# Spreading the fields of a compressed interaction network over partitions: DMA from a DRAM scratch in place of selection matmuls, with 17 split tiles in place of 23

## The reference

```python
for idx, (W, b) in enumerate(params):
    z = jnp.einsum('bhd,bkd,hks->bsd', x0, xk, W) + b[None, :, None]
    z = jax.nn.relu(z)
    if idx != n_layers - 1:
        half = z.shape[1] // 2
        xk = z[:, :half, :]
        direct.append(z[:, half:, :])
    else:
        direct.append(z)
logit = jnp.sum(jnp.concatenate(direct, axis=1), axis=-1)
```

## Time and profile before

| what | us |
|---|---|
| median of 3 runs | 2996.9 (2995.06 to 2997.92) |
| span of the profiled execution | 2989.2 |
| PE busy | 2879.6 (96%) |
| DVE busy | 2752.8 (92%) |
| ACT busy | 1724.0 (58%) |
| POOL busy | 1628.9 (54%) |
| bytes moved | 16.17 MB, 5 GB/s over the span |

### The profile page before, as it was taken

The page is one execution under the profiler, slowest core; times in us unless marked ns, Lnnn a source line. Parts: engine busy times, 40 slices in busy tenths (PEclk is TensorE's granted clock), DMA queues, the critical chain, the costliest instruction groups (busy, mean ns, idle before and its releaser), DMA issues.

```text
span 2989.2 us, 32998 instructions
## 1 busy us (share of the span) xinstructions
PE 2879.6 (96%) x9666; PEld 1773.7 (59%) x9666; DVE 2752.8 (92%) x2461; ACT 1724.0 (58%) x1733; POOL 1628.9 (54%) x644
## 2 busy tenths in 40 slices
PE   1999999999999999999999999999999999999988
PEld 0566665666666666666566666666666666666646
DVE  3599999999999999999999999999999999999983
ACT  0466655566655556665556666555666555566634
POOL 7448194783819566381965639396572948700000
PEclk9899999999999999999999999999999999999999
DMA  2000000000000000000000000000000000000000
GB/s 63 4 3 3 3 3 5 2 5 2 2 3 2 5 3 4 1 3 3 2 5 3 4 1 2 4 2 5 3 4 1 2 5 2 5 0 0 2 19 29
DMA packets 35184, 16.17 MB, mean 5 GB/s; under 512 B 17023, under 2 KB 33520, under 8 KB 35008
## 3 DMA queue, kind: packets, MB, share of 16 engines
q0 software_dynamic: 19968, 5.15, 2.0%
q1 hardware_dynamic: 11752, 7.61, 1.0%
q10 hardware_dynamic: 3367, 2.48, 0.3%
HBM read 13.09 MB, written 2.11 MB: 5 GB/s over the span
## 4 chain that ended last, share of the span: by engine, by line
PE 82%; ACT 6%; issue 5%; DVE 4%; ACTq 0%; POOL 0%; DMA 0%; SPq 0%; DVEq 0%
PE zacc_a L781 31%; PE zacc_b L781 26%; PE side_a L827 6%; PE side_b L827 6%; PE zacc_a L814 6%; PE zacc_b L814 5%; DVE prod L681 3%; ACT spread L508 2%; ACT high L527 1%; ACT direct L491 1%; ACT maps L490 1%; ACT maps L489 1%; DVE low L654 1%; DVE sums L690 1%; PE side_a L836 0%
## 5 line engine op out<-in xcount | busy, mean ns | idle before, releaser
L429 POOL DMA_INDIRECT landed<-in_tbl,rows_id x624 | 1527.4, 2448 | 203.8 <-issue 199.7
L681 DVE TENSOR_TENSOR prod<-spread,maps 128x1024 f32<-128x1024 f32 (+1 forms) x1280 | 1506.2, 1212 | 29.1 <-PE zacc_b L814 16.3
L527 ACT ACTIVATE high<-prod 128x1024 fp32r<-128x1024 f32 (+2 forms) x736 | 776.7, 1055 | 752.1 <-DVE prod L681 504.9
L654 DVE TENSOR_TENSOR low<-prod,high 128x1024 fp32r<-128x1024 f32 (+1 forms) x672 | 814.6, 1212 | 22.8 <-ACT high L527 22.7
L781 PE MATMUL zacc_a<-prod,w_plain 128*128 128x512 f32 (+2 forms) x1536 | 720.6, 594 | 0.0
L781 PE MATMUL zacc_b<-prod,w_plain 128*128 128x512 f32 (+2 forms) x1536 | 718.2, 593 | 0.0
L450 POOL TENSOR_TENSOR mark<-mark 128x1 f32<-128x1 f32 x15 | 101.1, 6743 | 770.7 <-DVE rows_split L608 697.0
L781 PEld LDWEIGHTS zacc_a<-prod,w_plain 128*128 128x128 f32 (+2 forms) x1536 | 289.7, 189 | 231.1 <-issue 201.2
L781 PEld LDWEIGHTS zacc_b<-prod,w_plain 128*128 128x128 f32 (+2 forms) x1536 | 289.1, 189 | 230.5 <-issue 197.0
L508 ACT ACTIVATE spread<-side_a 128x1024 f32<-128x1024 f32 x320 | 326.8, 1021 | 101.2 <-PE side_a L827 100.4
L508 ACT ACTIVATE spread<-side_b 128x1024 f32<-128x1024 f32 x320 | 327.0, 1022 | 89.3 <-PE side_b L827 78.1
(11 more groups left out here) (110 smaller groups left out, 1811.8 us busy)
## 6 DMA issues: line engine op xcount, KB each, us to landing
landed<-in_tbl,rows_id POOLq DMA_INDIRECT x624
features<-feat ACTq DMA_DIRECT2D x16, 128.0 KB, 1.7
spread<-features SPq DMA_DIRECT2D x4, 512.0 KB, 5.3
spread<-in_pick SPq DMA_DIRECT2D x1, 856.8 KB
spread<-in_W_top SPq DMA_DIRECT2D x1, 512.0 KB, 4.1
rows_id<-in_ids SPq DMA_DIRECT2D x16, 19.5 KB, 1.7
spread<-in_W_top SPq DMA_DIRECT2D x2, 128.0 KB, 2.8
spread<-in_W_top SPq DMA_DIRECT2D x1, 256.0 KB, 2.9
```

The source lines that it names most:

```text
L429: nc.gpsimd.indirect_dma_start(out=landed[:, f, :], out_offset=None, in_=tables[f], in_offset=bass.IndirectOffsetOnAxis(ap=rows_id[:, f:f ...
L527: nc.scalar.activation(high[0:rows, h, :], prod[0:rows, p, :], ACT.Copy).then_inc(s_round, 1)
L654: nc.vector.tensor_tensor(to, whole, top, ALU.subtract).then_inc(s_lowv, 1)
L681: nc.vector.tensor_tensor(to, spread[0:rows, t, :], maps[0:rows, :], ALU.mult).then_inc(s_prod, 1)
```

## The change

The selection matmuls, `pick`, the split of the rows and the ACT copies of spread tiles are gone. PE now turns the gathered rows in plain float32 (`turn_x`), both chunks of a group together at position 13 of an even turn, and ACT copies each to `x` (`copy_x`, position 15). SP then writes x to two scratch tensors in DRAM (`write_x`, position 16 of the even turn, for the two chunks that come two and three turns later): `x_copies`, 8 copies of even and odd fields, and `x_periods`, 4 copies of x in a row. From there SP loads what the products need: `load_first` (x_thrice in three DMAs, and the shifted x of u = 0 to 3) after the last product of layer 0, one `load_shifted` for each of u = 4 to 6, when a buffer of the ring of four is free, and ten `load_spread` of two tiles (1 MB) each, whose source repeats each row for 8 partitions. DVE multiplies the shifted x from SBUF. `PLAN` has 17 V tiles (7, 3 and 7 in the three parts) and 30 F tiles. GpSimd gathers all of a group from position 16 of an even turn on.

```diff
-PLAN = "FVFVFVFFVFVFFVFVFVFVFVFFFVFVFVFVFVVFVFVVFVFVFVV"
+PLAN = "FVFFVFFVFFVFFVFFFVFV" "FVFVFVF" "FVFFVFFVFFVFFVFFFVFV"
-LAG = 2
-AHEAD = 4
-LOW_ROWS_AT, COPY_ROWS_AT = 42, 40
-TURN_AT, THRICE_AT = 3, 9
+TURN_AT, COPY_AT, WRITE_AT, GATHER_AT = 13, 15, 16, 16
...
+    x_copies = nc.dram_tensor("x_copies", (GROUPS, 2, 2, COPIES, N1, COLS), f32, kind="Internal").ap()
+    x_periods = nc.dram_tensor("x_periods", (GROUPS, 2, PERIODS, FIELDS, COLS), f32, kind="Internal").ap()
...
-        pick = sb("pick", [SPLIT, PICK_W], f32r)
-        ident_r = sb("ident_r", [128, 128], f32r)
+        ident = sb("ident", [128, 128])
...
-            with sp.Fori(1, GROUPS) as g:
-                sp.wait_ge(s_gather, g * (16 * FIELDS))
-                sp.dma_start(rows_id[:, :], ids[bass.ds(g * ROWS, ROWS), :]).then_inc(s_ids, 16)
...
+            def write_x(n):
+
+                odd = n.odd
+                sp.wait_ge(s_x, n.count(1, 1))
+                for h in range(2):
+                    to = x_copies[bass.ds(group_of(n), 1), odd, h, :, :, :].rearrange("g i t c -> (g t) i c")
+                    sp.dma_start(to, x[h:EVEN:2, odd:odd + 1, :].to_broadcast([N1, COPIES, COLS])
+                                 ).then_inc(s_written[odd], 16)
+                to = x_periods[bass.ds(group_of(n), 1), odd, :, :, :].rearrange("g k f c -> (g f) k c")
+                sp.dma_start(to, x[0:FIELDS, odd:odd + 1, :].to_broadcast([FIELDS, PERIODS, COLS])
+                             ).then_inc(s_written[odd], 16)
+
+            def period(n, first, rows):
+                flat = x_periods[bass.ds(group_of(n), 1), n.odd, :, :, :].rearrange("g k f c -> (g k f) c")
+                return flat[first:first + rows, :]
+
+            def load_shifted(n, u):
+                rows = rows_of(N1 + u)
+                sp.dma_start(shifted[0:rows, u % RING0, :], period(n, PER0 * u, rows)).then_inc(s_shifted[u], 16)
+
+            def load_first(n):
+
+                sp.wait_ge(s_written[n.odd], n.group(48, 48))
+                for s in range(PER0):
+                    sp.dma_start(x_thrice[s * FIELDS:(s + 1) * FIELDS, :], period(n, FIELDS - s, FIELDS)
+                                 ).then_inc(s_thrice, 16)
+                for u in range(RING0):
+                    load_shifted(n, u)
+
+            def load_spread(n, q):
+                src = x_copies[bass.ds(group_of(n), 1), n.odd, :, :, PIECE * q:PIECE * (q + 1), :]
+                src = src.rearrange("g h i t c -> (g h i) (t c)")
+                to = spread[:, PIECE * q:PIECE * (q + 1), :].rearrange("p t c -> p (t c)")
+                sp.dma_start(to, src.unsqueeze(1).to_broadcast([2 * COPIES, COPIES, PIECE * COLS])
+                             ).then_inc(s_spread[q], 16)
+
+            def emit(turn, j):
+                nxt, after = turn.shift(1), turn.shift(2)
+                if turn.fixed and turn.number() == -1 and j == 0:
+                    write_x(nxt)
+                    write_x(after)
+                    sp.wait_ge(s_gather, 16 * FIELDS)
+                    sp.dma_start(rows_id[:, :], ids[ROWS:2 * ROWS, :]).then_inc(s_ids, 16)
+                    load_first(nxt)
+                if j == WRITE_AT and not turn.odd and after.real():
+                    write_x(after)
+                    write_x(turn.shift(3))
+                    if turn.shift(4).real():
+                        sp.wait_ge(s_gather, after.group(16 * FIELDS, 16 * FIELDS))
+                        sp.dma_start(rows_id[:, :], ids[bass.ds(after.group(ROWS, ROWS), ROWS), :]).then_inc(s_ids, 16)
+                u = j - N1 - 1 + RING0
+                if RING0 <= u < N0 and nxt.real():
+                    sp.wait_ge(s_square, nxt.count(N0, u - RING0 + 1))
+                    load_shifted(nxt, u)
+                if j == SQUARED[-1] and after.real():
+                    sp.wait_ge(s_square, nxt.count(N0, N0))
+                    load_first(after)
+                q = (j - LAST[0]) // PIECE
+                if j in LAST and (j - LAST[0]) % PIECE == PIECE - 1 and nxt.real():
+                    if turn.real():
+                        sp.wait_ge(s_prod, n_prod(turn, j) + 1)
+                    elif q == 0:
+                        sp.wait_ge(s_prep, 1)
+                    load_spread(nxt, q)
+
+            turns(sp, emit, GROUPS - 2)
...
+                fetched = turn.shift(4)
+                if j == GATHER_AT and not turn.odd and fetched.real():
+                    pool.wait_ge(s_ids, fetched.group(16, 16))
+                    pool.wait_ge(s_turned, fetched.count(1, 0))
+                    pool.wait_ge(s_mark, fetched.group(1, -1))
+                    nc.gpsimd.tensor_tensor(mark[:, 0:1], mark[:, 0:1], mark[:, 1:2], ALU.add).then_inc(s_mark, 1)
+                    gather()
...
-            def high_rows():
-
-                nc.scalar.activation(rows_split[:, :, 0:FIELDS].rearrange("p d f -> p f d"), landed[:, :, :], ACT.Copy
-                                     ).then_inc(s_rowh, 1)
-
-            def spread_tile(turn, t):
-
-                nxt = turn.shift(1)
-                rows = rows_of(t)
-                if turn.fixed and turn.number() == -1 and t == 0:
-                    act.wait_ge(s_prep, 1)
-                act.wait_ge(s_side, n_side(nxt, SPREAD_X + t) + 1)
-                if turn.real():
-                    act.wait_ge(s_prod, n_prod(turn, N1 + N0 + t) + 1)
-                nc.scalar.activation(spread[0:rows, t, :], side(nxt, SPREAD_X + t)[0:rows, :], ACT.Copy
-                                     ).then_inc(s_spread, 1)
+            def copy_x(n):
+
+                act.wait_ge(s_turned, n.count(1, 1))
+                if not n.fixed or n.number() > 1:
+                    act.wait_ge(s_written[n.odd], n.group(48, 0))
+                nc.scalar.activation(x[0:FIELDS, n.odd, :], sides[n.odd][0:FIELDS, :], ACT.Copy).then_inc(s_x, 1)
...
+                if j == COPY_AT and not turn.odd and turn.shift(2).real():
+                    copy_x(turn.shift(2))
+                    copy_x(turn.shift(3))
+                if nxt.real() and j == N1 + N0 - 1 + LZ:
+                    take(turn, 0)
...
-                        dve.wait_ge(s_thrice, nxt.count(1, 1))
-                    dve.wait_ge(s_side, n_side(nxt, SQUARE_X + u) + 1)
-                    nc.vector.tensor_tensor(to, side(nxt, SQUARE_X + u)[0:rows, :], x_thrice[0:rows, :],
+                        dve.wait_ge(s_thrice, nxt.count(16 * PER0, 16 * PER0))
+                    dve.wait_ge(s_shifted[u], nxt.count(16, 16))
+                    nc.vector.tensor_tensor(to, shifted[0:rows, u % RING0, :], x_thrice[0:rows, :],
                                             ALU.mult).then_inc(s_square, 1)
...
-                    dve.wait_ge(s_spread, turn.count(N1, t + 1))
+                    if t % PIECE == 0:
+                        dve.wait_ge(s_spread[t // PIECE], turn.count(16, 16))
...
-                def pick_fields(use, first, n):
-
-                    for hf in range(2):
-                        cols = slice(hf * BANK, (hf + 1) * BANK)
-                        done = nc.tensor.matmul(side(nxt, use)[0:n, cols], pick[:, first:first + n],
-                                                x_split[:, cols], start=True, stop=True)
-                    done.then_inc(s_side, 1)
...
+            def turn_x(n):
+
+                if not n.odd:
+                    pe.wait_ge(s_gather, n.group(16 * FIELDS, 16 * FIELDS))
+                if not n.fixed or n.number() > 1:
+                    pe.wait_ge(s_x, n.count(1, -1))
+                nc.tensor.matmul(sides[n.odd][:, 0:2], ident[:, :], ident[:, 0:2], start=True, stop=True)
+                for d in range(CHAN):
+                    done = nc.tensor.transpose(sides[n.odd][0:FIELDS, d * ROWS:(d + 1) * ROWS],
+                                               landed[:, :, n.odd * CHAN + d], ident[:, :])
+                done.then_inc(s_turned, 1)
...
+                if j == TURN_AT and not turn.odd and turn.shift(2).real():
+                    turn_x(turn.shift(2))
+                    turn_x(turn.shift(3))
```

More of the change, by code:

```diff
@@ L211, in build @@
         s_zero = sem("s_zero")
-        s_pick = sem("s_pick")
         s_prep = sem("s_prep")
@@ L708, in emit @@
                     low_part(then, i)
-                if j == LOW_ROWS_AT and not turn.odd and turn.shift(2).real():
-                    low_rows(turn.group(1, 2))
                 if turn.real() and j == N1 + LZ + 2:
```

168 lines of the change are left out of this document (44 added, 124 removed).

## The result

The changed kernel takes **3188.28 us** (median of 4 runs, 3169.29 to 3219.68) against 2997.41 for the kernel before on the same chip: **1.059 times, 95% interval 1.051 to 1.067, slower**. The prediction said 2870 us, 4% faster, with 2710 to 3090 as its range; the time lies outside. One of the four runs, 3219.68 us, was a slow one and is not in the ratio; the median of the other three is 3170.5.

The account below looks back on a forecast made before the run. PE and DVE, both nearly full, were taken as the bound, with a DMA wait of 4.5 us a chunk added. 196 + 31 x 83.5 + 79.8 + 7.7 = 2872, about 2870 us, 4% faster; range 2710 to 3090.

Parts of the forecast that it names:

- PE 77.5: PE's time per chunk, from 87.3 us, with selections and old turn off, six F tiles and new turn on.
- DVE 76.7: DVE's time per chunk, against 84.1 us before: 47 products, 17 low parts in place of 23, two reduces.
- 79 without a DMA wait: Chunk time in us with both engines within 1 us of each other, feeding each other through 8 buffers; floor 77.5.
- PE's turn: PE turning the gathered rows in plain float32: 2.0 us a chunk taken, against 0.55 for the old turn.
- The slack of 9.3 us: Even turns: time from the writes' issue until DVE needs the shifted x of u = 4, 15.9 less 6.6 us.
- The time of the writes: Even turns: 3.9 MB in 10.1 to 19.3 us plus 4.1 for the load; DVE waits 4.9 to 14.1, 9 taken.
- The third rival: The DMA is the bound (chance 0.17), by low rate or too few engines; with ten on x_copies writes, 3100 us.
- The start: Time to layer 2's first relu: from 202.9 to about 196 us, first product at 77 to 87, layer 1 about 104.
- The second rival, the lock-out: DVE's two-input SBUF operations lock GpSimd out, so gathers come late: 89.1 us a chunk, 3046 in all; chance 0.19.
- signs for the end of a lock-out: On GpSimd's gathers: two of 20.64 and 34.94 us ended at a DVE product out of PSUM and at a DVE gap.
- The spread loads: Loads of 1.05 MB taking 2.7 to 5.2 us, due about 30 us after issue, so hidden unless the queue runs full.
- the end: Time after layer 2's last relu, taken to keep its 79.8 us.

Follow-up runs that it names:

- after_one_copy: The changed kernel, but x_copies holds one copy of each row in place of eight and a spread load is two DMAs; 2852.47 us, ratio 0.956.
- more20: The changed kernel with ids loaded ahead of the six writes and 2.62 MB more written from 20 rows in every even turn; 3428.23 us, ratio 1.146.
- one_copy: The changed kernel with ids ahead, one chunk's writes at position 24 of every turn, load_first behind spread loads, x_copies of one copy; 2743.38 us, ratio 0.912.
- let_in: The kernel of one_copy with a short DVE reduce behind the products at positions 6, 13, 33 and 40 of every chunk; 2821.6 us, ratio 0.943.
- let_in_memset: The kernel of one_copy with a one-column DVE memset behind the products at the same four positions as let_in; 2737.52 us, ratio 0.914.

## Why the prediction was wrong, by its steps

- **PE 77.5, DVE 76.7, 79 without a DMA wait: nearly right.** Without the wait the chunk took 77.1. PE's turn was two pieces of 1.1 us for the group, from 1655.14 to the next matmul at 1657.10, 2.0 for two chunks and so 1.0 a chunk, not 2.0. That PE's and DVE's rings hide each other's waits was priced too high by 2 us.
- **The slack of 9.3 us: right.** The first write was issued at 1657.53, and DVE was through with the product before at 1667.5: 10.0 us.
- **The time of the writes: the step that failed.** The sum took 10.1 to 19.3 us from 386 and 202 GB/s, both reached by loads, and chose a wait of 9 by the middle. Writes and load took 36.7 us. By the rates of after_one_copy and more20, 12 GB/s an engine, the 2.6 MB from 20 rows need 22 us on ten engines and the 1.3 MB from 39 rows 8 us on thirteen: 30, and a load of 4 behind them make 34 of the 36.7. The third rival gave this case: writes of 29 us, a wait of 24, a chunk of 91, 3100 us. Measured were 26.7 and 91.5; that the chunk agrees so well is in part luck, since 79 was 2 too high and the late gathers, which that rival did not have, put 2.5 on. The Trainium skill's rule (DMA: Bandwidth & Descriptors, how many engines a DMA uses) is what the rival rested on, and the traces agree with it, as above. It should have had the sum and not a part of 0.17: nothing in the trace of before spoke against ten engines, and the case for the middle was the width of its own bounds.
- **The start: wrong by 59 us.** Predicted 196, measured 255.3. Layer 0's first product came at 101.0 us and not at 77 to 87, and layer 1's matmuls at 136.8 and not at 104: the chain there runs over the same writes and ten loads of 1 MB at 221 GB/s (from 116 to 162 us, the engines busy throughout), where 386 had been taken as possible. That is 33 of the 59. Another 22.6 is the wait at 209.56, which the prediction left out of the start though by its own mechanism it stands there too. With one copy it is 207.5, and with the ids ahead as well 199.9.
- **The second rival, the lock-out: its mechanism is there, its size was not.** 30 gathers over 20 us (996 us together) stand against 22 (654 us) in the kernel before, which hid them all. The late gathers cost 77 us, 2.5 a chunk, not 5.6, and went when the ids moved ahead of the writes, so that half of the gathers fell into DVE's waits. Its signs for the end of a lock-out, a gap of DVE or a product out of PSUM, are borne out by the traces; that a reduce between two-input operations lets GpSimd in is not, for the long ones.
- **The spread loads: right in the changed kernel, and near the edge.** The changed kernel's waits for them are 30 us in 7 places. They were priced by size; reading 16 rows eight times each costs a quarter of the queue's time against 128 rows, which shows once the 26.8 us are gone.

From the sum: 59 for the start, 31 x (91.5 - 83.5) = 248, less 2 for the end and 12 more between the median and this span than the 7.7 taken, make the 317 us from 2872 to 3188. The 12 are scatter: the profiled execution's own time is 1.8 us above its span, and the median of the four runs 17.8 above that time.

## What to carry to other kernels

- Before a transfer is priced by a rate, see from what shape that rate came: writes from 20 rows ran at 120 GB/s on ten engines and from 32 rows at 196 on sixteen, the same bytes. Give a DMA that others wait behind a slowest dimension that 16 divides.
- A queue is a line: the load that is needed next goes ahead of writes that are needed a turn later, and a burst is split. Moving the writes by eight positions, with the ids ahead of them and `load_first` behind the spread loads, turned 3188 into 2850 us, and halving the burst 2850 into 2766.
- A plan tuned with one set of operations is not worth the same with another: measure its part alone before crediting it (273 us the other way here).

## What the runs showed of the chip that was not expected

- With spread loads that read 16 DRAM rows eight times each the queue kept the engines busy 34% longer than with loads of the same size from 128 rows (2125 against 1585 us). With one row read 64 times (one_copy) the queue ran at 485.6 MB / (0.751 x 16 x 2745.2 us) = 14.7 GB/s a busy engine, near the 15.4 of eight times.
- Gathers that wait while DVE runs two-input SBUF operations do so for up to 36 us, through some 30 of them. The 47 of over 20 us in one_copy, let_in and let_in_memset all end 0.82 us after an idle gap of DVE of 0.03 us began, and have no other gap in them. The Trainium skill (SBUF — State Buffer, Who interferes with whom) says that a reduce never contends; it does not follow that one lets GpSimd in, as 34 reduces lie inside the 17 long gathers of let_in and ended none of them.
- The mean granted clock is 0.94 from 1500 to 1680 us where PE stands for some 27 us in two chunks, against 1.00 before: in the wait itself (1680 to 1700 us) it was 0.50, the lower level of 1.2 GHz, and it was at 0.89 in the 20 us before.
